# A gated cross-attention block on one core: keys of the first batch in three groups, row units spread over steps 0 and 1, the last batch divided per token, gates spread by matmul

## The chip, the cores and the metric

The kernel runs on one core of a Trainium2 chip. Its engines are TensorE (PE, matmuls; PEld are its weight loads), VectorE (DVE), ScalarE (ACT), GpSimd (POOL) and SyncE (SP), which here only issues DMAs. The metric is the device time of one execution in microseconds. Three executions of the kernel before took 1306.92, 1310.46 and 1322.75 us: the median is 1310.46.

## What is computed

The input x has 16 batches of 256 tokens of width 128; the context has 16 batches of 1601 keys of width 128. Cross-attention with 16 heads of depth 8, then a mixture of 8 experts (2 per token) with a shared expert, each behind a tanh gate:

```python
x = x + tanh(g_xattn) * attention(v=ctx, k=ctx, q=layernorm(x))
x = x + tanh(g_ffn) * ffn(layernorm(x))
# attention: softmax(qh @ kh.T / sqrt(8)) @ vh per head, then the dense projection
# ffn: scores = sigmoid(x @ gate_W) * route_scale; the top 2 of 8, normalised to sum 1,
#      weigh the experts gelu(x @ W1 + b1) @ W2 + b2; a shared expert is added
```

## The kernel before

A **step** is one group of eight heads (four pairs) of one batch: 32 steps, two per batch. A **chunk** is 512 tokens, that is two batches: 8 chunks. All that happens follows one list of events per step, ORDER[s], written as letters in PLAN; every engine walks through the same list and waits on counting semaphores.

The events:
- **S**, a row unit (`row_scores`, `maximum`): TensorE makes scores of 128 tokens against 512 keys for the two heads of a pair, in one of two b_ps banks, and VectorE takes their maxima. A step needs 26 of them: 24 of 512 keys and two for the 65 keys that are left. They run a step and ten units ahead (S_AHEAD).
- **T**: when the maxima of a step are complete they are negated, split in three bf16 parts, transposed by TensorE, copied by ScalarE into nm_t, and SyncE sends them as extra rows of q_op (`move_maxima`, 6 DMAs). Only then can the step's probabilities be made.
- **P**, a score pair: TensorE makes scores of 128 keys by 256 tokens with the maximum already taken off (four matmuls into two of three a_ps banks), ScalarE takes their exponential, 512 wide, into probs.
- **V** and **W**: TensorE multiplies probs with values into o_ps. Columns of ones in v_op also give the sums of the softmax. The last one of a step is followed by ScalarE's copy of o_ps into o_s.
- **A** units share the a_ps ring: K (project keys), V (project values), QT and QP (transpose and project normalised tokens), T, FT, FL, FG, FH (the feed-forward part: transpose, gate logits, transpose of gates, hidden layer). FH uses Gelu, P uses Exp: each change loads a table on ScalarE.
- **B** and **Y/Z** units share b_ps with S: D is the dense projection of a batch, Y and Z the two halves of the feed-forward output of 128 tokens.

Queries and keys are split into three bf16 parts, stored to memory (q_dram, k_dram) and loaded back in another layout (q_op, k_op, `load_operands`), four buffers deep. The keys of batches 1 to 15 are split by GpSimd (`split_keys`), those of batch 0 by VectorE (`split_run`), and the queries by GpSimd (`split_queries`). kctx and vctx hold one batch of context each, in one buffer each, so a load waits for the last projection from it.

The beginning, PROLOGUE, projects the keys of batch 0 in four runs of about 400 and the queries of chunk 0. VectorE and GpSimd fill k_op with ones first, because three rows of it have to stay one. SyncE stores all keys, ScalarE's queue all queries, and SyncE loads both. Then 26 row units run for step 0, T, the value projections of batch 0, QT and QP of chunk 1 and ten row units of step 1; after that come the first P.

The end: after the last P and V of step 31, the outputs of the last step go to memory (o_dram) and come back as num (the products) and den (the sums); den is inverted by VectorE, goes to memory once more (r_dram), comes back spread over the 128 partitions (den_all), and GpSimd multiplies (`divide`). The dense projection follows, then the output of chunk 6 (four Y/Z), the normalising of chunk 7 on GpSimd, its gates, whose result goes to memory and comes back spread (`spread_gates`, g_all), the hidden layer, GpSimd's product of both (`apply_gates`) and four Y/Z.

SyncE's queue is in order. In its loop over the steps it sends outputs, stores keys, loads operands, loads vctx, spreads sums and gates, moves maxima, loads kctx and stores queries, each behind a wait; what stands behind a wait has to wait too.

## Time and profile before

| | us |
|---|---|
| median of three executions | 1310.46 |
| profiled execution, its own time | 1312.06 |
| its span | 1310.3 |
| TensorE busy | 1183.9 (90%) |
| VectorE busy | 1068.6 (82%) |
| ScalarE busy | 1049.8 (80%) |
| GpSimd busy | 372.3 (28%) |

The page gives the busy time of each engine over the span and in 40 slices of 32.8 us. The timeline gives instructions in order of time, neighbours of one kind merged (x4: four instructions); an "SPq" or "ACTq" row is the issue of DMAs by that engine's queue. In brackets is how long the engine had been idle before, and what ended that. The chain is followed back from the last instruction to what released it at each step. The clock is the one granted to TensorE: 1.00 is 2.4 GHz, 0.50 is 1.2 GHz.

### The profile page before, as it was taken

How to read it: one execution, taken by the hardware profiler on the slowest of the kernel's cores; microseconds unless marked ns; L12 is line 12 of the kernel's file. 1: busy time of each engine (PE TensorE's matmuls, PEld its weight loads, DVE VectorE, ACT ScalarE, POOL GpSimd, SP SyncE). 2: the span in 40 equal slices, each digit the busy share in tenths (PEclk: the TensorE clock that was granted, in tenths of full speed). 3: DMA queues.
4: the chain of work that ended last, by engine and by line, in shares of the span. 5: the costliest groups of instructions: out<-in, count | busy, mean ns of one | idle time of the engine just before them, and what ended most of it. 6: DMA issues, size and time to landing. Idle time of an engine off the chain costs nothing.

```text
span 1310.3 us, 30858 instructions
## 1 busy us (share of the span) xinstructions
PE 1183.9 (90%) x11995; PEld 455.4 (35%) x11995; DVE 1068.6 (82%) x1337; ACT 1049.8 (80%) x1962; POOL 372.3 (28%) x361
## 2 busy tenths in 40 slices
PE   2369899989999999999999999999999999999854
PEld 1123333333333433343334433343333433343223
DVE  8478888989889898989898898879898899989011
ACT  1017897989998899988998899878998899889931
POOL 7424041421425042422424042422424032000111
PEclk7558998999999999999999999999999999999977
DMA  5854452635464654626363655636373654400101
GB/s 133 201 120 94 103 113 62 142 76 123 96 139 94 134 120 101 138 66 130 80 150 77 139 118 104 132 73 123 75 155 77 139 118 104 87 13 26 43 15 49
DMA packets 64100, 133.71 MB, mean 102 GB/s; under 512 B 13769, under 2 KB 38034, under 8 KB 60882
## 3 DMA queue, kind: packets, MB, share of 16 engines
q1 hardware_dynamic: 63090, 130.95, 46.2%
q8 instruction: 95, 1.56, 0.5%
q10 hardware_dynamic: 864, 0.79, 0.3%
q14 instruction: 51, 0.42, 0.1%
HBM read 87.91 MB, written 43.40 MB: 100 GB/s over the span
## 4 chain that ended last, share of the span: by engine, by line
PE 75%; DVE 10%; DMA 6%; ACT 5%; issue 2%; POOL 1%; SPq 1%; ACTq 0%; POOLq 0%; DVEq 0%
PE o_ps L792 30%; PE a_ps L774 18%; PE b_ps L758 13%; DVE run_max L917 7%; PE a_ps L706 5%; DMA vctx<-ctx_t 3%; PE a_ps L702 3%; ACT probs L586 3%; PE b_ps L737 2%; PE a_ps L698 1%; PE b_ps L726 1%; PE a_ps L685 1%; ACT L601 1%; DMA q_op<-q_dram 1%; PE b_ps L740 1%
## 5 line engine op out<-in xcount | busy, mean ns | idle before, releaser
L917 DVE TENSOR_REDUCE run_max<-b_ps 128x2 f32<-128x1024 f32 x768 | 899.0, 1218 | 126.0 <-PE b_ps L758 118.2
L586 ACT ACTIVATE probs<-a_ps 128x512 f32<-128x512 f32 (+1 forms) x1664 | 901.9, 595 | 105.2 <-PE a_ps L774 90.8
L792 PE MATMUL o_ps<-probs,v_op 128*32 128x256 f32 (+1 forms) x5368 | 501.9, 445 | 1.4 <-ACT probs L586 0.6
L758 PE MATMUL b_ps<-k_op,q_op 48*128 48x512 bf16 (+1 forms) x2048 | 317.1, 342 | 43.5 <-DVE run_max L917 24.6
L774 PE MATMUL a_ps<-q_op,k_op 51*128 51x256 bf16 (+1 forms) x3328 | 327.8, 275 | 18.7 <-ACT probs L586 15.0
L774 PEld LDWEIGHTS a_ps<-q_op,k_op 51*128 51x128 bf16 (+1 forms) x3328 | 108.0, 96 | 347.1 <-ACT probs L586 302.7
L792 PEld LDWEIGHTS o_ps<-probs,v_op 128*32 128x32 f32 x5368 | 107.4, 108 | 186.2 <-issue 113.0
L758 PEld LDWEIGHTS b_ps<-k_op,q_op 48*128 48x128 bf16 x2048 | 87.1, 95 | 164.9 <-DVE run_max L917 93.3
L488 POOL TENSOR_TENSOR k_parts<-k_t,one 128x400 bf16<-128x400 f32 (+1 forms) x60 | 51.4, 856 | 182.8 <-ACT k_t L607 182.8
L499 POOL TENSOR_TENSOR rstd_q<-rstd_q,minus_half 128x4 f32<-128x4 f32 x8 | 8.7, 1085 | 290.3 <-DVE rstd_q L850 290.3
L528 POOL TENSOR_TENSOR attn<-num,den_all 128x256 f32<-128x256 f32 x16 | 11.7, 729 | 236.7 <-PE b_ps L758 151.8
L607 ACT ACTIVATE k_t<-a_ps,bk_s 128x401 f32<-128x401 f32 (+1 forms) x64 | 38.4, 601 | 41.6 <-PE a_ps L702 41.2
L706 PE MATMUL a_ps<-wv_s,vctx 128*128 128x128 f32 (+1 forms) x416 | 63.9, 295 | 8.5 <-DMA vctx<-ctx_t 7.4
L702 PE MATMUL a_ps<-kctx,wk_s 128*128 128x400 f32 (+1 forms) x128 | 64.1, 594 | 5.9 <-DMA bk_s<-bk 5.9
L706 PEld LDWEIGHTS a_ps<-wv_s,vctx 128*128 128x128 f32 (+1 forms) x416 | 51.6, 194 | 27.7 <-ACT probs L586 15.0
L490 POOL TENSOR_TENSOR k_t<-k_t,k_parts 128x400 f32<-128x400 f32 (+1 forms) x60 | 56.9, 948 | 4.7
L494 POOL TENSOR_TENSOR k_parts<-k_t,k_parts 128x400 bf16<-128x400 f32 (+1 forms) x60 | 53.6, 893 | 4.7
L488 POOL TENSOR_TENSOR q_parts<-q_t,one 128x512 bf16<-128x512 f32 x8 | 8.4, 1045 | 161.9 <-ACT q_t L624 161.9
L492 POOL TENSOR_TENSOR k_parts<-k_t,one 128x400 bf16<-128x400 f32 (+1 forms) x60 | 51.0, 850 | 4.7
L612 ACT ACTIVATE v_op<-a_ps 128x512 f32<-128x512 f32 x64 | 33.0, 518 | 19.5 <-PE a_ps L706 19.0
L920 DVE TENSOR_REDUCE run_max<-b_ps 128x8 f32<-128x520 f32 x64 | 41.7, 694 | 3.3 <-PE b_ps L758 3.1
L534 POOL TENSOR_TENSOR hid<-hid,g_all 128x2048 f32<-128x2048 f32 x8 | 36.3, 4537 | 25.4 <-DMA g_all<-g_dram 17.6
(101 smaller groups left out, 612.0 us busy)
## 6 DMA issues: line engine op xcount, KB each, us to landing
k_op<-k_dram SPq DMA_DIRECT2D x64, 400.2 KB, 7.3
k_dram<-k_parts SPq DMA_DIRECT2D x32, 600.4 KB, 6.6
kctx<-ctx_t SPq DMA_DIRECT2D x16, 800.5 KB, 4.7
k_op<-k_dram SPq DMA_DIRECT2D x64, 200.1 KB, 7.8
vctx<-ctx_t SPq DMA_DIRECT2D x16, 800.5 KB, 11.0
o_dram<-o_s SPq DMA_DIRECT2D x32, 256.0 KB, 2.0
g_all<-g_dram SPq DMA_DIRECT2D x16, 512.0 KB, 6.0
k_dram<-k_parts SPq DMA_DIRECT2D x32, 200.1 KB, 5.8
```

What stands on the lines that cost most here:

```text
L488: pool.tensor_tensor(parts[0], whole, ones(whole, slice(0, whole.shape[0])), ALU.mult).then_inc(chain, 1)
L490: pool.tensor_tensor(whole, whole, parts[0], ALU.subtract).then_inc(chain, 1)
L492: pool.tensor_tensor(parts[1], whole, ones(whole, slice(0, whole.shape[0])), ALU.mult).then_inc(chain, 1)
L494: pool.tensor_tensor(parts[2], whole, parts[1], ALU.subtract).then_inc(chain, 1)
L586: act.activation(probs[0:keys, unit % PB, :], a_ps[at % AB][0:keys, :], ACT.Exp, scale=SCALE).then_inc(a_taken, 1)
L702: last = pe.matmul(bank[:, 0:n_keys], wk_s[:, :], kctx[:, k0:k0 + n_keys], start=True, stop=True)
L706: last = pe.matmul(bank[0:KEYS[t], 128 * (t % 4):128 * (t % 4) + 128], vctx[:, 128 * t:128 * t + KEYS[t]], wv_s[:, :], start=True, stop=True)
L758: last = pe.matmul(slot[:, side, to:to + n_keys], q_op[buf][rows, p, 128 * t:128 * t + 128], k_op[buf][rows, p, k0:k0 + n_keys], start=Tru ...
L774: last = pe.matmul(a_ps[(at + side) % AB][0:KEYS[t], SEQ * a:SEQ * a + SEQ], k_op[buf][rows, slot, 128 * t:128 * t + KEYS[t]], q_op[buf][r ...
L792: last = pe.matmul(o_ps[32 * j:32 * j + 32, cols], v_op[s // 2 % 2][0:KEYS[t], t, GP * (s % 2) + j, :], probs[0:KEYS[t], unit % PB, cols], ...
L917: dve.tensor_reduce(run_max[:, t, :, p, c:c + 1].rearrange("q v o -> q (v o)"), slot[:, :, :], AX.X, ALU.max).then_inc(b_taken, 1)
L920: dve.tensor_reduce(run_max[:, i - FULL, :, :, RUNS], slot[:, :, 0:GP * REST].rearrange("q v (p k) -> q v p k", p=GP), AX.X, ALU.max).then ...
```

## The change

It has two parts, at the beginning and at the end; steps 2 to 30 keep their lists.

**The beginning.** The context of batch 0 comes in three loads (512, 512 and 577 keys), the tokens of chunk 0 behind the first. Keys are projected in runs of 512, 512, 512 and 65 (KRUN_0). VectorE splits run 0, then the queries, then run 1; GpSimd splits runs 2 and 3. SyncE stores and loads the keys by group, in the order 0, 2, 1. The queries' stores are shared by ScalarE's queue (side 0) and GpSimd's queue (side 1), and GpSimd's queue also issues the two loads of step 0's queries. Ones are no longer filled by VectorE and GpSimd in k_op; a row of ones (k_row, 3 by 1601) is sent by eight DMAs. Step 0's 26 row units take key group 0 first, then 2, then 1 (`score_run`). The value projections of batch 0 and the key projections of batch 1 stand among them. The ten row units ahead are gone from there: six stand in step 0 and four in step 1 (`with_more_maxima`), and QT, QP of chunk 1 stand in step 0. The bias of values is folded behind T of step 0, in o_ps instead of b_ps.

**The end.** The output of chunk 6 stands in step 31's list. For batch 15 nothing goes to memory: the copied o_s is transposed by TensorE (unit OT, for step 30's half during step 31), VectorE inverts the sums and multiplies per token (`divide_tokens`), TensorE transposes back (unit AT), ScalarE copies, dense follows. Statistics of tiles 0 and 1 of chunk 7 are taken earlier, VectorE normalises chunk 7. The hidden layer stands ahead of the gates' transpose. The gates are spread by four matmuls with a constant pick_s, VectorE multiplies each quarter of hid, and the output's groups accumulate over the quarters in b_ps (`last_output`).

```diff
+KRUN_0 = [(RUN * c, RUN) for c in range(RUNS)] + [(RUN * RUNS, REST)]
+GROUPS = [(0, RUN), (RUN, RUN), (2 * RUN, CTX - 2 * RUN)]
+FIRST_RUNS = [0, 2, 1]
...
 def first_maxima():
...
+    events = [("S", n) for n in range(SUNITS)]
+    for i in range(4):
+        events.insert(events.index(("S", 3 * i + 3)), ("A", ("V", 0, i)))
+        events.insert(events.index(("S", 2 * i + 15)), ("A", ("K", 1, i)))
+    return events, [("A", ("T", 0, 0))]
...
+ORDER[0] = with_more_maxima(0, SUNITS, 6)
+ORDER[1] = with_more_maxima(1, 2 * SUNITS + 6, 4)
+ORDER[0].insert(len(ORDER[0]) // 4, ("A", ("QT", 1, 0)))
+ORDER[0].insert(len(ORDER[0]) * 2 // 5, ("A", ("QP", 1, 0)))
...
+    during = ORDER[STEPS - 1]
+    during.insert(len(during) // 3, ("B", ("OT", 0, 0)))
+    for i in range(4):
+        at = len(during) * (9 + i) // 14
+        during[at:at] = [("Y", ("FY", c - 1, i)), ("Z", ("FY", c - 1, i))]
+    ORDER[STEPS] = [e for e in ORDER[STEPS] if e[0] in "VW"] + [("B", ("OT", 1, 0)), ("A", ("AT", b, 0)),
+                                                               ("B", ("D", b, 0))]
+    ORDER[STEPS + 1] = [("A", ("FT", c, 0)), ("A", ("FL", c, 0))]
+    ORDER[STEPS + 2] = [("A", ("FH", c, i)) for i in range(GELU_TILES + 1)] + [("A", ("FG", c, 0))]
...
 # SyncE
-            store_keys(0)
-            load_operands(0)
+            store_group(0)
+            load_group(0)
+            store_group(2)
+            store_group(1)
+            load_group(2)
+            load_group(1)
             load_context("K", kctx, 1, kctx_in)
...
                 if s % 2 == 1 and 0 < b + 2 < BATCH:
                     store_keys(b + 2)
+                if s == -1:
+                    move_maxima(0)
                 if 2 <= s + 3 < STEPS:
                     load_operands(s + 3)
...
 # GpSimd
+            for i in (2, 3):
+                split_first_run(pool, k_second, i, 4 * (i - 2),
+                                lambda part, whole: pool.tensor_tensor(part, whole, ones(whole), ALU.mult))
+            store_queries(pool, 0, [1], q0_written)
+            load_queries(pool, 0, q0_in)
+            for i in range(2):
+                pool.memset(v_op[i][:, :, :, 16:32], 1.0).then_inc(v_ones, 1)
...
 # VectorE, the end
+            def divide_tokens(h):
+                unit = b_ps[B_SLOT["OT", h, 0]][:, 0, :].rearrange("q (i j r) -> q i j r", i=4, r=32)
+                dve.wait_ge(b_filled, b_done("OT", h))
+                dve.reciprocal(sum_inv[:, :, :], unit[:, :, :, 16]).then_inc(inv_seq, 1)
+                dve.wait_ge(inv_seq, h + 1)
+                for side in range(2):
+                    last = dve.tensor_tensor(attn_tok[:, :, side, h], unit[:, side::2, :, DH * side:DH * side + DH],
+                                             sum_inv[:, side::2, :].unsqueeze(3).broadcast_to([128, QTILES, GP, DH]),
+                                             ALU.mult)
+                last.then_inc(b_taken, 1)
+            def last_output():
+                for m in range(GELU_TILES):
+                    dve.wait_ge(pick_filled, m + 1)
+                    dve.tensor_tensor(hid[:, m, :], hid[:, m, :], a_ps[m % AB][:, :], ALU.mult).then_inc(pick_taken, 1)
```

**SyncE, from the six token loads on, before.** The waits in brackets are semaphores: k_chain is the split of batch 1's keys, a_taken the copy of step 0's maxima.

```order
L337 DMA x_s<-x 128x512 x6
L427 DMA k_dram<-k_parts 64x3x1601 [waits k_chain]
L429 DMA k_dram<-k_parts 64x1601
L427 DMA k_dram<-k_parts 64x3x1601
L429 DMA k_dram<-k_parts 64x1601
L362 DMA k_op<-k_dram 32x6404 [waits q_written,k_written,k_ones2]
L362 DMA k_op<-k_dram 16x6404
L364 DMA q_op<-q_dram 48x4x256
L362 DMA k_op<-k_dram 32x6404
L362 DMA k_op<-k_dram 16x6404
L364 DMA q_op<-q_dram 48x4x256
L437 DMA q_op<-nm_t 1x4x256 [waits a_taken]
```

And of the change, from the same place on:

```order
L455 DMA x_s<-x 128x512 x6
L551 DMA k_dram<-k_parts 64x3x1601 [waits k_chain]
L553 DMA k_dram<-k_parts 64x1601
L551 DMA k_dram<-k_parts 64x3x1601
L553 DMA k_dram<-k_parts 64x1601
L579 DMA q_op<-nm_t 1x4x256 [waits a_taken]
L579 DMA q_op<-nm_t 1x4x256 x5
L484 DMA k_op<-k_dram 32x6404 [waits k_written]
```

The maxima rows of step 0 have moved ahead of step 2's operands, and stay behind the store of batch 1's keys. kctx of batch 2 follows step 2's operands.

**TensorE, from T of step 0 (into 24 columns' rows, nm_parts) to the first key projection of batch 2 (kctx, 128x401), before.** b_ps rows are row units (two matmuls each), rows of four a_ps<-q_op,k_op are one P.

```order
L712 MATMUL a_ps<-ident_b,nm_parts 24x128 x2
L706 MATMUL a_ps<-wv_s,vctx 128x128 x4
L682 MATMUL a_ps<-ident,xn_q 128x128 x4
L706 MATMUL a_ps<-wv_s,vctx 128x128 x8
L706 MATMUL a_ps<-wv_s,vctx 65x128
L758 MATMUL b_ps<-k_op,q_op 128x512 x10
L685 MATMUL a_ps<-xn_t_q,wq_s 128x512
L758 MATMUL b_ps<-k_op,q_op 128x512 x10
L774 MATMUL a_ps<-q_op,k_op 128x256 x4
L758 MATMUL b_ps<-k_op,q_op 128x512 x2
L774 MATMUL a_ps<-q_op,k_op 128x256 x4
L758 MATMUL b_ps<-k_op,q_op 128x512 x2
```

And of the change:

```order
L883 MATMUL a_ps<-ident_b,nm_parts 24x128 x2
L831 MATMUL o_ps<-ident,bv_p 128x128
L833 MATMUL o_ps<-wd_s,bv_t 128x128
L992 MATMUL a_ps<-q_op,k_op 128x256 x4
L974 MATMUL b_ps<-k_op,q_op 128x512 x2
L992 MATMUL a_ps<-q_op,k_op 128x256 x4
L974 MATMUL b_ps<-k_op,q_op 128x512 x2
L992 MATMUL a_ps<-q_op,k_op 128x256 x4
L974 MATMUL b_ps<-k_op,q_op 128x512 x2
L873 MATMUL a_ps<-kctx,wk_s 128x401
```

Ten row units, the value projections and QT, QP stand no longer between T and the first P; the two matmuls of the bias do.

**TensorE, from the last product with values to the end, of the change.** Before, dense, four output groups, FT, FL, FG, five FH and four output groups stood here in this order, without the rows of o_s, attn_tok and pick_s.

```order
L910 MATMUL b_ps<-ident,o_s 128x128 x4
L852 MATMUL a_ps<-ident,attn_tok 128x128 x2
L900 MATMUL b_ps<-wd_s,attn 128x128 x2
L845 MATMUL a_ps<-ident,xn_f 128x128 x4
L857 MATMUL a_ps<-gate_s,xn_t_f 128x8 x4
L866 MATMUL a_ps<-xn_t_f,w_s 128x512 x4
L866 MATMUL a_ps<-xn_t_f,ws_s 64x512
L862 MATMUL a_ps<-ident,g_tok 8x128 x4
L922 MATMUL a_ps<-hid_s,pick_s 128x512
L937 MATMUL b_ps<-ws_s,hid_s 128x128 x4
L922 MATMUL a_ps<-hid_s,pick_s 128x512
L928 MATMUL b_ps<-w_s,hid 128x128 x4
```

The first four output groups have moved up into step 31, and the hidden layer ahead of the gates' transpose.

## Rows read from the trace of the kernel before

**Rows 1.** The page, the granted clock in 40 slices of the span:

```profile
PEclk7558998999999999999999999999999999999977
```

**Rows 2.** Busy time by stretch: start:end, length, busy us of each engine, clock, DMA:

```profile
102.50:141.00 38.50, 36.68 (x344) 13.44 (x342) 31.34 (x32) 30.86 (x59) 14.14 (x16) 0.94 0.37 73
141.00:174.60 33.60, 29.30 (x342) 9.40 (x338) 29.72 (x31) 29.90 (x58) 0.00 (x0) 1.00 0.59 128
1224.00:1259.00 35.00, 27.97 (x312) 7.23 (x308) 0.00 (x0) 32.28 (x62) 0.00 (x0) 1.00 0.03 11
1300.00:1305.00 5.00, 4.81 (x22) 4.81 (x23) 0.49 (x2) 0.00 (x0) 0.14 (x1) 0.50 0.02 5
1305.00:1310.00 5.00, 2.44 (x20) 2.25 (x18) 0.92 (x3) 0.00 (x0) 0.00 (x0) 0.95 0.14 52
```

**Rows 3.** Timeline of the beginning up to the first row unit: start, us, engine, line:

```profile
7.45 0.81 DVE L843 BATCH_NORM_STATS2 stats_q<-x_s 128x6 f32<-128x128 f32 x4
9.64 0.37 DVE L946 CAST k_parts<-k_t 128x401 bf16<-128x401 f32 x1 [0.77 <-ACT k_t L607]
10.66 1.09 DVE L950 CAST k_parts<-k_t 128x401 bf16<-128x401 f32 x1
15.33 0.69 ACT L624 ACTIVATE q_t<-a_ps,bq_s 128x512 f32<-128x512 f32 x1 [1.28 <-PE a_ps L685]
19.82 1.36 POOL L494 TENSOR_TENSOR q_parts<-q_t,q_parts 128x512 bf16<-128x512 f32 x1
21.22 7.69 ACTq L321 DMA_DIRECT2D q_dram<-q_parts  x6
45.92 1.04 PE L758 MATMUL b_ps<-k_op,q_op 48*128 48x512 bf16 x4 [17.22 <-DMA q_op<-q_dram]
```

**Rows 4.** Timeline on to the first P and K2.0; last row: DMAs, us to landing:

```profile
52.12 4.98 PE L702 MATMUL a_ps<-kctx,wk_s 128*128 128x401 f32 x8
57.46 21.59 DVE L917 TENSOR_REDUCE run_max<-b_ps 128x2 f32<-128x1024 f32 x19 [3.68 <-PE b_ps L758]
69.14 0.89 POOL L494 TENSOR_TENSOR k_parts<-k_t,k_parts 128x400 bf16<-128x400 f32 x1
73.68 1.12 SPq L429 DMA_DIRECT2D k_dram<-k_parts  x1
79.52 0.80 SPq L362 DMA_DIRECT2D k_op<-k_dram  x2
82.30 3.85 SPq L437 DMA_DIRECT2D q_op<-nm_t  x6
86.20 0.44 SPq L417 DMA_DIRECT2D kctx<-ctx_t  x1
98.91 0.63 PE L774 MATMUL a_ps<-q_op,k_op 51*128 51x256 bf16 x4
102.48 1.71 PE L702 MATMUL a_ps<-kctx,wk_s 128*128 128x401 f32 x2
...
kctx<-ctx_t SPq DMA_DIRECT2D x1, 800.5 KB, 7.7
```

**Rows 5.** The chain that ended last, its end, and one row of ScalarE's timeline:

```profile
1258.97 0.60 ACT o_s L594
1280.64 0.20 ACT score L626
1284.69 0.20 DVE g_tok L887
1286.08 0.59 ACT hid_s L631
1288.83 6.68 DMA g_all<-g_dram
1307.48 0.35 DVE y_s L904
...
1291.77 0.68 ACT L635 ACTIVATE hid_s<-a_ps,bs_s 64x512 f32<-64x512 f32 x1 [0.32 <-PE a_ps L698]
```

More of the change, by code:

```diff
@@ L146, in first_maxima, with with_more_maxima, last_steps @@
 def first_maxima():
-    scores = [event for event in ORDER[-2] if event[0] == "S"]
-    rest = [event for event in ORDER[-2] if event[0] != "S"]
-    first = [event for event in ORDER[-1] if event[0] == "S" and event[1] < SUNITS]
-    turn = [("A", ("T", 0, 0))]
-    return scores[:5] + rest + scores[5:], first + turn + [e for e in ORDER[-1] if e not in first + turn]
-ORDER[-2], ORDER[-1] = first_maxima()
+    events = [("S", n) for n in range(SUNITS)]
[3 more added lines that the diff above has]
+    return events, [("A", ("T", 0, 0))]
+def with_more_maxima(s, n, more):
+    turn, last = ("A", ("T", s + 1, 0)), SUNITS * (s + 2) - 1
+    events, seen, due = [], 0, 0
+    for kind, unit in ORDER[s]:
+        if kind == "S":
+            events.append(("S", n))
+            n, seen = n + 1, seen + 1
+            due += seen % (SUNITS // more) == 0 and seen // (SUNITS // more) <= more
+        elif (kind, unit) != turn:
+            events.append((kind, unit))
+            if kind == "P" and due:
+                events.append(("S", n))
+                n, due = n + 1, due - 1
+    events.insert(events.index(("S", last)) + 5, turn)
+    return events
+ORDER[-2], ORDER[-1] = first_maxima()
+ORDER[0] = with_more_maxima(0, SUNITS, 6)
+ORDER[1] = with_more_maxima(1, 2 * SUNITS + 6, 4)
+ORDER[0].insert(len(ORDER[0]) // 4, ("A", ("QT", 1, 0)))
+ORDER[0].insert(len(ORDER[0]) * 2 // 5, ("A", ("QP", 1, 0)))
+def last_steps():
+    c, b = CHUNKS - 1, BATCH - 1
+    during = ORDER[STEPS - 1]
[7 more added lines that the diff above has]
+    ORDER[STEPS + 2] = [("A", ("FH", c, i)) for i in range(GELU_TILES + 1)] + [("A", ("FG", c, 0))]
+    for s in range(STEPS + 3, LAST + 1):
+        ORDER[s] = []
+last_steps()
 def step_of(unit):
@@ L329, in load @@
                 return sp.dma_start(dst[tuple([slice(None)] * len(src.shape))], src)
-            load(kctx, ctx_t[0]).then_inc(kctx_in, 16)
-            for dst, src in keys:
-                load(dst, src).then_inc(key_in, 16)
             def load_tokens(c0, c1, arrived):
@@ L469, in _ @@
                     sp.dma_start(out[:, 4 * c:4 * c + 4, :], y_s[:, :, :]).then_inc(out_done, 16)
-            sp.wait_ge(out_done, 16 * CHUNKS)
+            for i in (0, 2):
+                sp.wait_ge(y_done, i + 2)
+                sp.dma_start(out[:, TILES - 4 + i:TILES - 2 + i, :], y_s[:, i:i + 2, :]).then_inc(out_done, 16)
+            sp.wait_ge(out_done, 16 * (CHUNKS + 1))
         @block.gpsimd
@@ L685, in a_unit @@
                     last = pe.matmul(bank[:, :], wq_s[:, :], xn_t["q"][:, :], start=True, stop=True)
+                elif kind == "AT":
+                    pe.wait_ge(b_taken, b_done("OT", 1))
+                    for t in range(QTILES):
+                        last = pe.transpose(bank[:, 128 * t:128 * t + 128],
+                                            attn_tok[:, t].rearrange("q s h j d -> q (s h j d)"), ident[:, :])
                 elif kind == "FL":
@@ L837, in fold_bias, with statistics @@
                 dve.wait_ge(bias_seq, 4)
-            def statistics(w, c):
+            def statistics(w, c, tiles=range(4)):
                 seq = lambda k: dve.wait_ge(bn_seq[w], 6 * c + k)
-                for t in range(4):
+                for t in tiles:
                     dve.bn_stats(stats[w][:, t, :], x_s[:, 4 * c + t, :]).then_inc(bn_seq[w], 1)
+                if tiles[-1] < 3:
+                    return
                 seq(4)
@@ L1005, in _ @@
                     gates = []
+            last_output()
 def kernel(**inputs):
```

336 lines of the change are left out of this document (238 added, 98 removed).

## The prediction

> **What bounds the kernel now.** I read the page first, then the busy time by stretch, then the timelines of the beginning and the end. TensorE's clock row is at the full level in the middle slices and lower in the first four and the last two [rows 1]: the change works on exactly these two ends. In the middle three engines are close together: between 102.5 and 174.6 us TensorE is busy 66.0 of 72.1 us, VectorE 61.1, ScalarE 60.8 [rows 2]. A row unit (two matmuls, one VectorE maximum) moved into a step therefore meets no idle engine. Step 31, the last, has no row units: ScalarE is busy 32.3 of 35 us, TensorE 28.0, VectorE 0 [rows 2].
>
> Beginning, to be read as a chain: token statistics 7.45, queries projected 15.33 + 0.69, split on GpSimd until 21.18, stored by ScalarE's queue until 28.9, and the first row unit at 45.92 [rows 3]. Then 26 row units, the key projection of batch 1 at 52.12, its split until 70.03, its store until 74.8, maxima rows sent from 82.30, and the first probabilities' matmul only at 98.91 [rows 4]. Between 82.3 and 98.9 stand value projections and ten row units for step 1. The end is one chain of 51.3 us, from the last copy of sums at 1258.97 to the span's end at 1310.3 [rows 5]; 24 us of it lie behind the gates' copy at 1286.08.
>
> **Step A, the first row unit.** Tokens are loaded ahead of most keys and VectorE no longer fills k_op: the statistics can begin when the tokens land instead of at 7.45. 800 KB of keys now come in three loads and only the first is ahead of the tokens; I take 5.3, a gain of 2.2. The projected queries are then ready at 16.0 - 2.2 = 13.8. VectorE splits them in four operations instead of GpSimd's 5.1 us (16.02 to 21.18). The same cast took 0.37 us alone and 1.09 beside a GpSimd operation [rows 3]; GpSimd now splits key group 2 at that time, so four operations cost between 2.5 and 5; I take 4.4, because GpSimd is busy for most of it: ready at 18.2, before at 21.18. The Trainium skill (SBUF — State Buffer, Who interferes with whom) says that a VectorE cast in its two-port mode and a GpSimd operation lock each other out for the whole instruction; the two casts agree with this.
>
> From ready queries to the first row unit took 24.7 us before [rows 3]. ScalarE's six stores took 7.69; now three go there and three on GpSimd: -3.8. The load needs the queries and one third of the keys, not all keys, and has a queue of its own. No row shows a DMA issued by GpSimd. Its price lies between ScalarE's 1.28 us per issue and, if five of them stand in line behind other work, some 3 us each. I take 14.8 us from ready to first row unit: **33 us** (28 to 42; 42.9 if the stretch stays 24.7). Before: 45.9. The key groups come after that: group 2 is needed 8 units later, group 1 16 units later, and I put their landing at 36 and 41, 8 us early.
>
> **Step B, from there to step 0's first key projection.** A row unit costs VectorE 21.59/19 = 1.136 us [rows 4]. Four value projections (about 2.1 us at the low clock) and four key projections now stand among them; two banks hold 2.3 us of VectorE's work, so each costs 0 to 0.8: 2.4 in sum. Batch 1's first key projection comes after 15 units: 33 + 17.0 + 2.4 = 52.4. Before it was at 52.12. From there the same work follows: 17.9 us to the end of the split, 4.8 to the end of the store [rows 4]. The maxima of step 0 are ready at 33 + 26 units + 2.4 + 0.9 = 65, before at 81.9. But SyncE now has the store of batch 1's keys ahead of the maxima rows, and waits there for GpSimd's split, to 70.3. The rows leave at 75.1 to 79 and the first probabilities' matmul is at about 80.5 instead of 98.9. The gap of 15 us between 65 and 80 is this change's new wait.
>
> Second wait: the first three pairs of step 0 take 3.6 us (98.91 to 102.48), then TensorE wants keys of batch 2 (K2.0). Their load is issued behind the operands of step 2, which wait for the keys' store to land (4.7 us after its last issue) and take 2.7: 82.5, before at 86.20. It landed 7.7 us after issue [rows 4]; right behind 1.4 MB of operand loads I add 1.8: 92. TensorE gets there at 84 and stands 8 us, with everything queued behind it: the row units, so VectorE, and the pairs, so ScalarE. K2.0 at 92 against 102.48: **-10.5**. Both waits hang on GpSimd's split and move with step A.
>
> **Step C, ten row units in steps 0 and 1, with QT and QP of chunk 1.** In TensorE's time a row unit is about 0.32 us in the dense part: 3.2, and the query projection about 1.5: 4.7. In VectorE's time ten cost 11.4 us, against 7.2 + 3.9 idle in the two stretches [rows 2]. So at least +4.7, at most +11.4; both engines end near full, which they never pack: I take **+7**. At the end of step 1: -10.5 + 7 = -3.5.
>
> **Step D, the end.** All of chunk 6's outputs (4 groups of ten matmuls; 20 matmuls took 2.44 us at 0.95 of the clock [rows 2], so 1.2 each) and one transpose unit go into step 31, whose TensorE has 7 us idle; four bunches in a ring of three banks, so not for nothing: +1.5 (0 to 5). After the last sums: copy 0.60, transposes 0.65, reciprocal and two products 0.8, transposes and copy 0.95, dense 1.0, add 0.5, statistics of two tiles 1.15, power 1.1, four normalising operations on VectorE 0.9, transposes 0.65, copy 0.7, logits 1.15, exponential 0.25: 10.4. Hidden layer now ahead of the gates' copy: from the table load to the last Gelu 5.8 us (1286.7 to 1292.45), which hides the 4.0 us of gate arithmetic (1280.84 to 1284.88); the copy 0.6: 16.8. Then four spreading matmuls, four products of 0.7 and 20 output groups: TensorE's 8.4 us at the full clock, up to 15 at the low one. Output groups ran at a granted clock of 0.50, the 1.2 GHz level, in 1300 to 1305, after 6 us without TensorE work, and at 0.95, nearly all at 2.4 GHz, behind that [rows 2]; I take 9.8: 26.6. Last addition 0.35, output 2.15: **29.1** (27.5 to 33), before 51.3. Gone are the trips through memory: 9 us for sums and 9 us for gates (6.68 of it one row) and the 4.5 us GpSimd product. D: -22.2 + 1.5 = **-20.7**.
>
> The Trainium skill (TensorE: Matmul & The Clock Gate, Part 1) says that the low clock is the default and activity lifts it; by this rule the end, now denser, would take 27.5 to 29 us. The rows of 1300 to 1310 agree with it.
>
> **Sum.** -3.5 - 20.7 = -24.2 from the profiled execution's own 1312.06: 1287.9. The median of the runs shown is 1.6 lower: **1286 us**, 1.9% less.
>
> **Rivals.**
> (1) Faster than that: GpSimd's DMAs cost like ScalarE's and queries land early (first unit at 28, -5), row units fill idle time (+4.7 instead of +7), the end at 27.5 (-1.6), step 31 takes its guests free (-1.5): 1286 - 10.4 = 1276. For it: VectorE is idle 11 us in the two stretches of steps 0 and 1 [rows 2]. Against: both waits of step B, which stay in this case too.
> (2) GpSimd's DMAs are slow, the first unit at 42, and step B moves with it: 1286 + 9 + 2 = 1297. The Trainium skill (SBUF — State Buffer, SBUF: two separate sides) says that a VectorE copy in two-port mode keeps GpSimd from writing descriptors. Here VectorE's casts of key group 1 run just then; five issues each held for one cast of 1.09 us are 5.5 us late.
> (3) Chunk 6 in step 31 isn't hidden and the end stays at the low clock: +3.5 and +4: 1293.
> (4) Slower than before: the same queue as in (2), but starved until the key stores are over. Everything hangs on it one for one; it decides from a first row unit at 33 + 24 = 57 us, 11 later than before. At 84, which 2% slower needs, nothing in the trace points.
>
> **How the numbers follow.** Forecast 0.48, (1) 0.27, (2) 0.13, (3) 0.09, (4) 0.03. The range reaches from (1) with 3 us more to (2) with 2 more: 1273 to 1299. 2% of 1310.46 is 26 us (about what a measurement of this kernel can tell), so the border is 1284.3. Above 2% faster: all of (1) and 0.15 of the forecast, whose own range is 1279 to 1293: 0.42. Slower by 2%: 0.01. The rest 0.57.
>
> **What would show it.** Step A: the first row unit at 28 to 42. B: SyncE's store of batch 1's keys ahead of the maxima rows, VectorE idle from about 65 to 80, TensorE waiting for kctx near 84 to 92. C: sums' copy of step 1 at 171, before 174.6. D: 29 us from the last sums' copy to the end. If VectorE has no gap at 65, B is wrong and the time is below 1280; if the end takes over 35 us, D is.

## The result and the profile after

The changed kernel takes 1306.15 us in the median of 20 runs (1300.64 to 1315.73), the kernel before 1315.69 in 20 runs beside it (1306.92 to 1328.52): the ratio is 0.9932, 95% interval 0.9912 to 0.9953. Forecast were 24 us less; it is 9.5, or 0.7%. The profiled execution took 1310.04 us (span 1308.2); the one before had 1312.06, so these two traces differ by 2.0 us only.

The timeline of the beginning, kernel after (start, us, engine, line; to be read beside [rows 3, 4]):

```profile
13.35 0.69 ACT L788 ACTIVATE q_t<-a_ps,bq_s 128x512 f32<-128x512 f32 x1 [1.28 <-PE a_ps L848]
24.63 1.18 POOL L428 DMA_DIRECT2D q_op<-q_dram  x2 [3.47 <-DMA q_dram<-q_parts]
28.74 1.04 PE L974 MATMUL b_ps<-k_op,q_op 48*128 48x512 bf16 x4 [15.43 <-DMA q_op<-q_dram]
...
70.32 6.18 SPq L579 DMA_DIRECT2D q_op<-nm_t  x6
78.16 0.61 PE L992 MATMUL a_ps<-q_op,k_op 51*128 51x256 bf16 x4 [11.87 <-DMA q_op<-nm_t]
79.23 3.79 DVE L1175 TENSOR_REDUCE run_max<-b_ps 128x2 f32<-128x1024 f32 x3 [10.49 <-PE b_ps L974]
90.34 1.68 PE L873 MATMUL a_ps<-kctx,wk_s 128*128 128x401 f32 x2 [8.59 <-DMA kctx<-ctx_t]
133.95 0.60 ACT L756 ACTIVATE o_s<-o_ps 128x512 f32<-128x512 f32 x1
174.15 0.60 ACT L756 ACTIVATE o_s<-o_ps 128x512 f32<-128x512 f32 x1
```

The first row unit comes 17 us sooner and batch 2's first keys (K2.0) 12.1 us sooner. The last two rows, the copies of the sums of steps 0 and 1, tell what is left: 7.1 us at the end of step 0 (141.04 before) and 0.4 us at the end of step 1 (174.58).

The timeline of the end, kernel after (to be read beside [rows 5]):

```profile
1269.44 0.60 ACT L756 ACTIVATE o_s<-o_ps 128x512 f32<-128x512 f32 x1 [1.26 <-PE o_ps L1010]
1278.55 1.09 PE L845 MATMUL a_ps<-ident,xn_f 128*128 128x128 f32 x4 [4.18 <-DVE xn_f L1083]
1282.11 6.31 PE L866 MATMUL a_ps<-xn_t_f,w_s 128*128 128x512 f32 x8
1290.17 0.58 ACT L795 ACTIVATE hid_s<-a_ps 8x512 f32<-8x512 f32 x1
1290.81 1.12 PE L922 MATMUL a_ps<-hid_s,pick_s 8*128 8x512 f32 x2 [0.85 <-ACT hid_s L795]
1295.81 2.07 PE L922 MATMUL a_ps<-hid_s,pick_s 8*128 8x512 f32 x2
1301.81 3.78 PE L928 MATMUL b_ps<-w_s,hid 128*128 128x128 f32 x16
```

From the last copy of sums to the span's end are 38.8 us (51.3 before). The same spreading matmul took 1.12 us at 1290.81 and 2.07 at 1295.81. Busy time by stretch of this end (start:end, length, busy us, clock, DMA):

```profile
1268.00:1270.00 2.00, 1.06 (x8) 0.16 (x8) 0.00 (x0) 0.74 (x2) 0.00 (x0) 1.00 0.00 0
1276.00:1278.00 2.00, 0.00 (x0) 0.00 (x0) 0.81 (x4) 0.00 (x0) 1.01 (x1) 0.50 0.00 0
1292.00:1294.00 2.00, 2.00 (x11) 1.12 (x11) 0.66 (x1) 0.00 (x0) 0.00 (x0) 1.00 0.00 0
1296.00:1298.00 2.00, 2.00 (x3) 0.50 (x4) 0.09 (x1) 0.00 (x0) 0.00 (x0) 0.50 0.00 0
```

The granted clock is 0.50 (1.2 GHz) from 1270.4 to 1287.4 and again from between 1294 and 1295 to the end, the second time although TensorE has had work without a gap since 1290.81. Step 31 takes 33.6 us (28.9 before), and steps 2 to 30 together 1061.7 against 1055.5.

### The profile page after: what moved, and what is told of

Same layout as the page of the kernel before. It is cut to its first block, busy times and chain, and to the rows that moved or that the text cites. A ratio compares the mean times of both kernels' runs of the same rounds, so it can differ in the third digit from the quotient of the medians.

```text
span 1308.2 us, 30941 instructions
## 1 busy us (share of the span) xinstructions
PE 1200.6 (92%) x12013; PEld 460.2 (35%) x12013; DVE 1060.5 (81%) x1343; ACT 1051.0 (80%) x1963; POOL 357.3 (27%) x366
## 4 chain that ended last, share of the span: by engine, by line
PE 71%; DVE 8%; DMA 6%; issue 5%; ACT 3%; POOL 3%; SPq 2%; POOLq 0%; ACTq 0%; DVEq 0%
PE o_ps L1010 27%; PE a_ps L992 16%; PE b_ps L974 12%; DVE run_max L1175 6%; PE a_ps L877 5%; DMA vctx<-ctx_t 3%; PE a_ps L873 3%; ACT probs L748 2%; PE a_ps L866 2%; PE b_ps L951 2%; DMA kctx<-ctx_t 1%; DMA r_dram<-den 1%; PE b_ps L900 1%; ACT L763 1%; PE a_ps L857 1%
## 5 line engine op out<-in xcount | busy, mean ns | idle before, releaser
L992 PE MATMUL a_ps<-q_op,k_op 51*128 51x256 bf16 (+1 forms) x3328 | 328.6, 276 | 30.0 <-ACT probs L748 14.8
L873 PE MATMUL a_ps<-kctx,wk_s 128*128 128x400 f32 (+3 forms) x128 | 66.3, 604 | 13.0 <-DMA kctx<-ctx_t 8.6
L877 PEld LDWEIGHTS a_ps<-wv_s,vctx 128*128 128x128 f32 (+1 forms) x416 | 53.0, 198 | 30.2 <-issue 17.4
L769 ACT ACTIVATE k_t<-a_ps,bk_s 128x401 f32<-128x401 f32 (+2 forms) x64 | 38.4, 602 | 22.1 <-PE a_ps L873 21.6
L866 PE MATMUL a_ps<-xn_t_f,w_s 128*128 128x512 f32 x64 | 34.1, 661 | 1.1 <-ACT hid L797 0.3
## 6 DMA issues: line engine op xcount, KB each, us to landing
vctx<-ctx_t SPq DMA_DIRECT2D x16, 800.5 KB, 10.8
```

The costliest lines, as they stand in the source:

```text
L866: last = pe.matmul(to, w, xn_t["f"][:, :], start=True, stop=True)
L873: last = pe.matmul(bank[:, 0:n_keys], wk_s[:, :], kctx[:, k0:k0 + n_keys], start=True, stop=True)
L877: last = pe.matmul(bank[0:KEYS[t], 128 * (t % 4):128 * (t % 4) + 128], vctx[:, 128 * t:128 * t + KEYS[t]], wv_s[:, :], start=True, stop=True)
L992: last = pe.matmul(a_ps[(at + side) % AB][0:KEYS[t], SEQ * a:SEQ * a + SEQ], k_op[buf][rows, slot, 128 * t:128 * t + KEYS[t]], q_op[buf][r ...
```

## Experiments

Times are medians, with the ratio to before and its 95% interval. Before was run again beside each kernel (medians 1313.37 to 1317.03 us), so kernels are compared by the ratios. The changed kernel's own ratio is 0.9932 (0.9912 to 0.9953); where another's interval overlaps this one, the whole time doesn't tell the two apart, and what is said rests on a part of one profile of each. "Sums 1" is the start of the copy of step 1's sums; "tail" runs from the copy of step 31's sums to the span's end.

### Which end brought the gain

```diff
-last_steps()
...
-            last_output()
```

With these two calls goes all that serves the new end; before's end stands in its place.

> The changed kernel with its old end: the last batch divided by the spread sums, the gates spread through DRAM, chunk 6's outputs in step 33, last normalisation on GpSimd; the beginning is the new one. Theory (from the two traces): the beginning is worth little by the end of step 1 (174.15 us against 174.58), so this kernel stands within 3 us of before (1310 to 1316 in the medians), its sums of step 1 are copied at 173 to 175, its step 31 takes 28.9 us again instead of 33.6, and its tail is about 51 us. The end is then worth 6 to 9 us. Rival: the end gave nothing (its tail's 12 us are eaten by step 31 and by the low clock) and the beginning the 9 us: this kernel would stand at 1304 to 1308.

Measured: 1314.49 us, ratio 1.0003 (0.997 to 1.0036). Sums 1 at 173.28, step 31 28.87 us, tail 51.7. The beginning alone is worth nothing that shows, and its interval lies clear of the changed kernel's: the end brought the 0.7%, 12.9 us in the tail less 4.7 in step 31. The rival, 1304 to 1308 us, is refuted.

### The beginning: ten units, and the wait for kctx

```diff
-ORDER[0] = with_more_maxima(0, SUNITS, 6)
-ORDER[1] = with_more_maxima(1, 2 * SUNITS + 6, 4)
+ORDER[0] = [("S", n) for n in range(SUNITS, SUNITS + S_AHEAD)] + ORDER[0]
```

> The changed kernel, but the ten row units ahead stand in front of step 0 (between the turn of the first maxima and the first scores) as they did before, instead of being spread over steps 0 and 1. Theory: steps 0 and 1 are lengthened by these ten units (43.6 and 40.2 us against 38.6 and 33.5 before), and VectorE's idle 10.5 us ahead of the first scores takes them for nothing: steps 0 and 1 go back to about 39 and 34 us, the clock doesn't fall at 168 to 178 us, and the end of step 1 comes 8 to 11 us sooner (163 to 166), the whole 8 to 11 us faster than the changed kernel. Rival: the steps are longer for another reason (the wait for kctx, transfers, the clock), or the ten units delay the first scores as much as they save: end of step 1 within 2 us of 174, whole within 0.3%.

The second edit, kctx_early, loads batch 2's context ahead of the store of batch 1's keys (and no longer behind step 2's operands):

```diff
+                if s == -1:
+                    load_context("K", kctx, 2, kctx_in)
                 if s % 2 == 1 and 0 < b + 2 < BATCH:
                     store_keys(b + 2)
```

> The changed kernel, with the load of batch 2's context (kctx) issued ahead of the store of batch 1's keys instead of behind the loads of step 2's operands. Theory: TensorE's 8.59 us wait at the first keys of batch 2 (90.34 us) goes: those keys at 81 to 83, the end of step 0 7 to 8.6 us sooner (125 to 127 against 133.95). By the end of step 1 the rest of it may be lost again, since VectorE's row units fill that step: 166 to 170 against 174.15, whole 4 to 8 us faster. Rival: the wait is taken over by the next one (VectorE's row units, or the keys' copy): end of step 1 within 2 us, whole the same.

The sums' copies, first two rows of ten_in_gap, in the second fence of kctx_early, whose K2.0 stands ahead of them:

```profile
130.55 0.60 ACT L755 ACTIVATE o_s<-o_ps 128x512 f32<-128x512 f32 x1
164.08 0.60 ACT L755 ACTIVATE o_s<-o_ps 128x512 f32<-128x512 f32 x1
```

```profile
82.67 1.71 PE L875 MATMUL a_ps<-kctx,wk_s 128*128 128x401 f32 x2
126.20 0.60 ACT L758 ACTIVATE o_s<-o_ps 128x512 f32<-128x512 f32 x1
166.39 0.60 ACT L758 ACTIVATE o_s<-o_ps 128x512 f32<-128x512 f32 x1
```

ten_in_gap: 1298.64 us, ratio 0.9897 (0.9854 to 0.994). Step 1 is 33.5 us again and sums 1 comes 10.1 us sooner (8 to 11 expected). From K2.0 to sums 1 are 74.0 us (90.05 to 164.08) instead of 83.8: this is what the ten units cost in these two steps, 9.8 us, the fall of the clock behind them (below) included. kctx_early: 1298.91, ratio 0.9889 (0.9846 to 0.9931). K2.0 no longer waits, and both copies come 7.8 us sooner: nothing of it is lost by the end of step 1. In the profiles both theories hold at the sizes expected. In the whole time each interval overlaps the changed kernel's; only both edits together (all_three, below) are clear of it.

Is it VectorE that the ten units cost, or TensorE? Two kernels with cheaper maxima. VectorE reads only half of the columns, in half_max for 20 units and in half_wide for all 62 units of steps 0 and 1 (there `if SUNITS <= n < 3 * SUNITS + 10`):

```diff
-... slot[:, :, :],
+                    seen = RUN // 2 if 0 <= n - SUNITS < 10 or 0 <= n - 2 * SUNITS - 6 < 10 else RUN
+... slot[:, :, 0:seen],
```

> The changed kernel, but twenty row units (the first ten that run in step 0 and the first ten of step 1's list) are reduced by VectorE over half their columns, about 0.55 us each instead of 1.09; TensorE's matmuls and the order stay. The row maxima then miss half of those keys (the subtracted number is another, which the division takes out again). Theory: the ten units added to steps 0 and 1 cost their full time on VectorE, 43.6 + 40.2 against 38.6 + 33.5 us before, since VectorE is busy in nearly every window of these steps: with 5.5 us less for VectorE in each, step 0 is 3.5 to 5.5 and step 1 3.5 to 6 us shorter (end of step 1 at 163 to 167 against 174.15). Rival: TensorE's share of the units (0.39 us each, and the waits of the scores queued behind them) lengthens the steps: end of step 1 at 172 to 174.

Measured: 1307.26, ratio 0.9918 (0.9891 to 0.9946); sums 1 at 173.12, 1.0 us sooner only, and K2.0 1.5 us sooner, so from K2.0 on nothing is gained. My theory missed. VectorE's busy time fell from 76.8 to 67.8 us between 78 and 182, and TensorE's waits for row maxima hardly changed (3.8 us, 4.0 in the changed kernel): they stand at other units. The reason may be that the two banks hand VectorE at most two units ahead, so that time saved at a unit that nobody waits for isn't kept for later ones; no run shows this by itself.

> The changed kernel, but all 62 row units that run in steps 0 and 1 are reduced by VectorE over half their columns (0.55 us instead of 1.09), not only the first ten of each step; the row maxima then miss half of those keys (the subtracted number is another, which the division takes out again). The run before (twenty units) moved nothing, with TensorE's waits for VectorE at 3.8 us as before: they stand at other units. Theory: of the 11.7 us by which steps 0 and 1 are longer, TensorE's waits for VectorE's row units are about 4 us and the fall of the clock behind the last of them 2 to 3; the rest is TensorE's own matmuls of the ten units. With all units at half time the waits go, the clock stays up: step 1 35 to 37 us instead of 40.2, step 0 1 to 2.5 us shorter, end of step 1 at 166 to 170. Rival: TensorE's own work and order is all of it: end of step 1 at 172 to 174.

TensorE's waits for row maxima between 98 and 166 us, in the changed kernel and in half_wide (us in total, times, longest):

```profile
PE b_ps L974 <- DVE run_max L1175: 4.0, 9, 0.9
```

```profile
PE b_ps L974 <- DVE run_max L1176: 0.6, 2, 0.4
```

Measured: 1295.37, ratio 0.9868 (0.9837 to 0.9899); sums 1 at 162.87, 11.3 us sooner, more than my 4 to 8. Step 1 took 34.4 us, 0.9 above before's, the clock stayed at 1.00 behind its last bunch, and K2.0 came 2.6 us sooner. From K2.0 to sums 1 are 75.1 us, 8.7 less than in the changed kernel and 3.0 more than before. So the larger part of the lengthening hangs on VectorE's time; my expectation had given nearly half of it to TensorE's own matmuls. VectorE's price of the ten units alone can't be read from this run: all 62 units were shortened, so part of the 8.7 us is time that before paid as well. Here the whole time too is clear of the changed kernel's.

Behind the last bunch of units the clock fell (168 to 178). In step1_busy the matmuls of step 1's last four row units are done three times, to fill TensorE's waits there:

```diff
-for p, to, k0, n_keys in parts:
+for p, to, k0, n_keys in parts * (3 if 3 * SUNITS + 6 <= n < 3 * SUNITS + 10 else 1):
```

> The changed kernel, but the last four row units of step 1's list (units 84 to 87, behind which TensorE waited 0.5 to 0.7 us each for VectorE) do their matmuls three times over before VectorE may read them, with the same values. Theory: step 1 lasts 40.2 us and not 36 to 37 because TensorE's waits at these units let the granted clock fall to 0.50 from 168 to 178 us; with the waits filled the clock stays at 1.00 and step 1 takes 36.5 to 38.5 us, step 2 1 us less. Rival: VectorE's row units hold the step's end, and the fall of the clock hits where nothing waits for TensorE, or comes anyway: step 1 stays at 39.5 to 41 us.

Stretches of the changed kernel, and in the second fence of step1_busy:

```profile
166.00:168.00 2.00, 0.74 (x8) 0.18 (x4) 2.00 (x3) 1.07 (x2) 0.00 (x0) 0.96 0.53 218
168.00:170.00 2.00, 2.00 (x10) 0.30 (x10) 2.00 (x2) 0.00 (x0) 0.00 (x0) 0.50 0.00 0
```

```profile
166.00:168.00 2.00, 1.67 (x16) 0.65 (x16) 2.00 (x3) 1.07 (x3) 0.00 (x0) 1.00 0.75 301
168.00:170.00 2.00, 1.69 (x16) 0.37 (x14) 2.00 (x3) 0.39 (x1) 0.00 (x0) 1.00 0.00 0
```

Measured: 1305.04, ratio 0.9915 (0.9882 to 0.9948), not told apart from the changed kernel. The clock stayed at 1.00, step 1 took 38.3 us instead of 40.2 and step 2 39.3 instead of 40.7. That fits, but is not shown by it: of six profiles of kernels with exactly the changed kernel's beginning, four had the fall (step 1 40.2 us in the changed kernel, begin_only, warm_tail and spread73) and two had not (37.9 in y_late and after_again). The fall costs about 2.3 us in step 1 and 1 to 3 in step 2, and whether it comes differs from run to run, with the kernel unchanged too (the changed kernel and after_again).

### Step 31 and the tail

```diff
-        during[at:at] = [("Y", ("FY", c - 1, i)), ("Z", ("FY", c - 1, i))]
...
+    ORDER[STEPS + 2][-1:-1] = late[0] + late[1]
+    ORDER[STEPS + 2] += late[2] + late[3]
```

Units 0 and 1 stand behind the hidden matmuls, 2 and 3 behind the gates' turning (FG). The last chunk's hidden values go to g_all and its gates to a tensor of their own (end_s), because chunk 6's are still in use.

> The changed kernel, but chunk 6's outputs are computed in the tail, where TensorE waits for the GELUs and the gates, not in step 31; the last chunk's hidden values and gates then lie in tensors of their own (g_all, and one more) so that chunk 6's are not overwritten. Theory: in step 31 TensorE is full already (about 1.08 us a pair of scores), so four bunches of 1.3 us lengthen it by 4.7 us (33.6 against 28.9); in the tail they are hidden. Step 31 goes back to 28.9 to 29.5 us, the tail stays at 38.8 (+0 to 1.5), whole 3.5 to 5 us faster. Rival: step 31 is long because VectorE or the turning of the sums holds it, or the tail grows by as much: whole within 1.5 us.

Measured: 1302.43, ratio 0.9906 (0.9872 to 0.9941). Step 31 took 28.89 us: chunk 6's four bunches cost all of the 4.7 us. But the tail grew from 38.8 to 42.6, more than I allowed: at the low clock TensorE had no gap behind the hidden matmuls (1270.19 to 1277.5 in one run of work), so the units pushed the gates' turning from 1277.5 to 1279.8 and the first spreading behind that. Of the 4.7 us gained, 3.8 are lost again, and the ratio doesn't tell this kernel from the changed one. This profile holds one thing more. From 1270.19 on TensorE works without a gap, and the clock comes back to 1.00 at 1276; it falls all the same at 1286, some 3 us after the first spreading matmul (1282.58):

```profile
1284.00:1286.00 2.00, 2.00 (x11) 1.12 (x10) 0.55 (x2) 0.00 (x0) 0.00 (x0) 0.96 0.30 113
1286.00:1288.00 2.00, 2.00 (x9) 1.78 (x10) 0.56 (x1) 0.00 (x0) 0.00 (x0) 0.50 0.00 0
```

In warm_tail 22 matmuls whose result nobody reads stand in the tail's waits:

```diff
+def keep_busy(times):
+    for _ in range(times):
+        pe.matmul(o_ps[:, :], ident_b[:, :], k_parts[:, 0, 0:512], start=True, stop=True)
```

> The changed kernel with matmuls added in the tail whose result nobody reads (bf16, 128 rows by 512 columns, into the bank of the sums, which is free by then): 2 after each turning of the sums and of the attention, 10 after the last dense product, 2 after the turned normalised tokens, 1 after the gates' turning, 1 ahead of each of the four groups of the output. Theory: the tail is 38.8 us and not 29 because TensorE's granted clock fell to 0.50 as soon as TensorE waited between 1269 and 1278, and the tail's matmuls then took twice the time; kept busy it stays at 1.00, the hidden matmuls take about 3.7 us instead of 7.4, the tail is 30 to 33 us, the whole 6 to 9 us faster. Rival: the clock falls in the tail for another reason (the kind of matmuls that run there), or the chain of ScalarE and VectorE holds the tail: the clock falls all the same, the tail stays at 38 to 43 us, the whole is the same or up to 3 us slower for the added matmuls.

```profile
1274.00:1276.00 2.00, 1.65 (x12) 1.18 (x12) 0.00 (x0) 0.60 (x1) 0.00 (x0) 0.95 0.00 0
1276.00:1278.00 2.00, 2.00 (x6) 1.44 (x7) 0.86 (x4) 1.18 (x2) 0.00 (x0) 0.50 0.00 0
1290.00:1292.00 2.00, 2.00 (x7) 1.47 (x7) 0.00 (x0) 0.00 (x0) 0.00 (x0) 0.50 0.00 0
```

Measured: 1305.79, ratio 0.9928 (0.9898 to 0.9957), tail 39.3 us: nothing. These are stretches of warm_tail. The clock was at 1.00 again from 1270, behind the added matmuls. After 2.03 us without work ahead of 1273.9 and 0.35 more it fell before the hidden matmuls, and it fell a second time just before 1290 in the output's part, where TensorE had been at work without a gap since 1285.7. Waits alone don't explain the tail. What differs there is the kind of matmul: the spreading has 8 rows of operands. So spread73 gives it 72, the 64 added ones against zeros:

```diff
-pe.matmul(a_ps[m % AB][:, :], pick_s[HID:HID + EXPERTS, m, :], g_t, ...)
+pe.matmul(a_ps[m % AB][:, :], pick_w[:, m, :], hid_s[0:HID + EXPERTS, :], ...)   # upper 64 rows zero
```

> The changed kernel, but the last chunk's gates are spread by matmuls over 72 rows (the 8 rows of gates and the 64 above them, against zeros) instead of over 8; columns, count and result are the same. Theory: in the tail the granted clock falls to 0.50 at 1294 although TensorE is busy in every window, because the matmuls there use few of the rows; with 72 rows it stays at 1.00 to the end, and the output's part (15.2 us from the first spreading to the last matmul) takes 9 to 11 us, the whole 4 to 6 us less. Rival: rows don't matter, it is the short matmuls of the output (128 columns, each with a load of weights) that let the clock fall, or the earlier waits: the clock falls at the same place, the whole is the same within 0.3%.

Timeline and stretches of spread73 (72 rows, in spite of the label):

```profile
1285.25 1.13 PE L926 MATMUL a_ps<-hid_s,pick_w 72*128 72x512 f32 x2 [0.85 <-ACT hid_s L798]
1290.61 1.02 PE L926 MATMUL a_ps<-hid_s,pick_w 72*128 72x512 f32 x2
1291.47 2.10 PE L932 MATMUL b_ps<-w_s,hid 128*128 128x128 f32 x16
```

```profile
1288.00:1290.00 2.00, 2.00 (x14) 1.52 (x13) 0.77 (x2) 0.00 (x0) 0.00 (x0) 1.00 0.00 0
1292.00:1294.00 2.00, 1.57 (x13) 1.30 (x11) 1.35 (x5) 0.00 (x0) 0.00 (x0) 1.00 0.00 0
```

Measured: 1299.00, ratio 0.9871 (0.9803 to 0.994); tail 32.4 us. From the first spreading to the last output matmul are 8.3 us instead of 14.8, at a clock of 1.00 throughout. As many matmuls with as many columns, only with 72 rows of operands instead of 8: the theory holds. The rival (the short output matmuls, or the earlier waits) falls: both are still there. The intervals of the whole time overlap, so this rests on the profiles, but on all of them: in the eleven with 8 rows the clock fell in this part every time (12.7 to 15.9 us), in the three with 72 rows (spread73, all73, all73_warm) never (8.2 to 8.3 us).

### The edits together

> The changed kernel with the ten row units ahead in front of step 0, batch 2's context loaded before batch 1's keys are stored, and chunk 6's outputs taken out of step 31 into waits of the tail (one behind the turned sums, two behind the last dense product, one behind the gates; last chunk's hidden values in tensors of their own). Theory: the three gains are of different causes, of which the first two share the wait ahead of step 0's keys: end of step 1 at 156 to 159 us (164.1 with the first alone, 166.4 with the second), step 31 28.9 us, tail 39 to 41 us, whole 15 to 20 us faster than the changed kernel in the medians. Rival: both edits of the beginning take away the same wait: end of step 1 at 163 to 165, whole 10 to 13 us faster.

Measured: 1283.43, ratio 0.9752 (0.9699 to 0.9806). Sums 1 at 155.00, 19.2 us sooner: the two gains of the beginning (10.1 and 7.8) add up, and this profile lacks the clock's fall in step 1. Step 31 took 30.2 us, not the 28.9 expected; the clock fell there at 1219 for some 4 us. The tail took 35.2, less than expected; its output's part was 12.7 us.

> As the kernel of three edits, and the first maxima's six transfers issued ahead of the store of batch 1's keys: they are ready at 64.3 us but issued at 70.3, behind a store that waits for GpSimd's split. Theory: first scores at 72 to 73 instead of 78.2, and step 1 ends 4 to 6 us sooner than with three edits. Rival: by then VectorE is at its ten row units until 76 us and holds the first steps anyway, or the store of the keys comes late for the operands of step 2: within 1.5 us of three edits.

Measured: 1282.43, ratio 0.9769 (0.9727 to 0.9811), sums 1 at 155.50: the rival. The six transfers left at 64.36, but TensorE waits for VectorE between the ten row units ahead of step 0, so the first scores came at 77.9 (77.4 in all_three).

> The kernel of three edits (ten units ahead of step 0, batch 2's context early, chunk 6's outputs in the tail) with the gates spread over 72 rows, the upper 64 of the matrix of picks set to zero in place. Theory: the clock stays at 1.00 in the output's part, which takes 8 to 9 us; tail 31 to 33 us against 35.2, whole 1277 to 1281, 24 to 30 us faster than the changed kernel in the medians. Rival: with chunk 6's output among the turned gates the clock fell at another place (1273.9) and for another reason: 1282 to 1285.

Measured: 1276.49, ratio 0.9709 (0.9675 to 0.9742), the fastest: 2.9% below before, the first with its whole interval more than 2% below, and by the two ratios some 2.2% below the changed kernel. From all_three its interval is not clear. In its profile the clock was at 1.00 from 1242 to 1256 and from 1264 to the end, tail 30.8 us; one fall stays, ahead of the hidden matmuls.

> As the kernel before it, and four added matmuls (bf16, 128 rows by 512 columns, nobody reads them): one after the turned attention, three after the turned normalised tokens. Theory: they fill the waits of 0.6 and 0.8 us after which the clock fell at 1260, the hidden matmuls run at 1.00 (about 4 us instead of 5.4 and 1.1), and the tail is 1 to 2.5 us shorter than without. Rival: the gates' product (8 columns a matmul) lets the clock fall by itself, or the GELUs and the gates' chain (4 us behind the scores) hold this part: within 0.5 us, or 0.5 us longer.

Measured: 1279.05, ratio 0.9733 (0.9698 to 0.9768): no gain. The hidden matmuls ran at 0.50 in 1258 to 1262 all the same. The waits of 0.6 and 0.8 us ahead of them were filled, so these are not what lets it fall there, or not alone. But the longest wait, 1.95 us for VectorE's normalised tokens, ends 1 to 2 us ahead of the fall in both kernels, and neither it nor the gates' product was tested alone; this is left open. The tail, 32.4 us, also holds a fall at its head (1247 to 1250) that all73's profile doesn't have.

> The changed kernel once more, for a second profile of it. Theory: the 4.8 us lost in its step 4 (a 3.4 us wait for vctx with the clock at 0.53 for 4 us) is the luck of one run, so step 4 is 36 to 37 us here and steps 2 to 30 together about 1057 us as in before, against 1061.7 in the first profile; step 1, with VectorE's last units, is either 38 (clock stays) or 40.2 us (clock falls), as in the kernels with the same beginning; step 31 33.6 us; tail 38 to 40 us. Rival: the change causes the loss of step 4: it is 41 us again.

Time of this run 1308.41. Step 4 took 36.8 us (41.2 in the first profile), steps 2 to 30 1055.7: the 6.2 us that the middle seemed to lose are luck of the first profile, 4.8 of them in step 4 and 1.5 in step 2, behind the fall at 168. But its step 31 took 38.6 us (33.6 in the first), because there the clock was low:

```profile
1238.00:1242.00 4.00, 4.00 (x22) 1.18 (x20) 0.04 (x1) 2.46 (x5) 0.00 (x0) 0.50 0.01 2
```

This fall lasted from 1231 to 1244 and cost 5.0 us; TensorE's waits around its start, up to 1.08 us, stand in the first profile too, without a fall. Step 4 of the first profile is another case. There TensorE first waited for vctx, and the clock fell in that wait, from 270 to 277:

```profile
271.56 2.05 PE L877 MATMUL a_ps<-wv_s,vctx 128*128 128x128 f32 x8 [3.37 <-DMA vctx<-ctx_t]
```

The same wait was 1.49 us in after_again, without a fall, and 3.79 in all73, whose step 4 took 41.4 us. So single profiles differ by more than some of the edits do.

## Why the prediction was right and wrong

What failed is above all step D. It took chunk 6's units as nearly hidden in step 31 (+1.5), and it priced the tail's matmuls at the full clock (29.1 us). The runs show +4.7 and, with the low clock in both halves of the tail, 38.8. Step C was mis-sized as well, by 4.7 us.

**Step A** put the first row unit at 33; it came at 28.74, in rival (1)'s place. Queries were ready at 14.0 (13.8 forecast), VectorE's split ended at 17.9 (18.2). From the split's end to the first unit it took 10.8 us, not 14.8: GpSimd's issues, the unknown, took 0.59 to 0.66 us each, as much as ScalarE's own 0.66 in this kernel and half of its 1.28 of before. Rival (2) never arose, and no issue of GpSimd's is seen to wait for a cast of VectorE's. One reading was loose: the cast of 0.37 us called alone (9.64) ran beside a small operation of GpSimd's (9.02 to 10.05, 128x4), so the trace agrees with a lock between the two only for the large ones.

**Step B** was right in its mechanism: the store of batch 1's keys ahead of the maxima rows, VectorE idle for 10.5 us, then TensorE's wait for kctx, 8.6 us (8 forecast). K2.0 came at 90.34, 12.1 us sooner (10.5 forecast). The runs add what the forecast left out: the gap of 10.5 us was the place for the ten units (ten_in_gap), and the second wait could be taken away by the order of one load (kctx_early). VectorE's gap was 10.5 us and not 15 because folding the bias and the statistics of chunk 1 came first, until 68.7, and the first scores came at 78.16 already (80.5 forecast).

**Step C** is a mis-sized term: +7 forecast, +11.7 measured (steps 0 and 1 from K2.0: 83.8 against 72.1). The forecast holds 5.5 us for the ten units and 1.5 for QT and QP. The ten units cost 9.8 us (ten_in_gap), and the 1.9 us that ten_in_gap still has above before are left for QT and QP. About 2.3 of the 9.8 are the clock's fall behind the last bunch, which no term held; without a fall (y_late, after_again) the two steps cost 8.4 and 10.7 us more than before, inside my bounds of 4.7 and 11.4. So the units themselves cost some 7.5 us, an estimate from these numbers, two thirds of VectorE's full time of 11.4. I had chosen by the average idle time of VectorE, 11 us, as if most of it could be used; about 4 us could. The end of step 1 gained 0.4 to 2.7 us in the six profiles, not 3.5, and where the clock fell step 2 gives most of it back or more: it ends 0.2 to 2.0 us later than before's (begin_only 0.3), where it didn't, 0.8 and 2.4 us sooner.

**Step D** holds most of the miss: -20.7 forecast, -7.9 measured (-12.6 in the tail, +4.7 in step 31).
- Step 31, 3.2 us: I counted 7 us idle in TensorE's row [rows 2]. But this time lies in pieces. A pair's scores and values mostly take TensorE 0.96 of the 1.08 us that ScalarE takes for them, which leaves gaps of 0.12 us, and its longer waits for ScalarE are five, of at most 1.1 us (3.8 in sum). Before:

```profile
1240.61 0.39 PE L774 MATMUL a_ps<-q_op,k_op 51*128 51x256 bf16 x4
1240.93 0.64 PE L792 MATMUL o_ps<-probs,v_op 128*32 128x256 f32 x8
1241.69 0.39 PE L774 MATMUL a_ps<-q_op,k_op 51*128 51x256 bf16 x4
```

  A bunch of 1.3 us fits into none of them. After the change ScalarE waits 1.12 us at a bunch; y_late, without them, is back at 28.89:

```profile
1256.85 2.17 ACT L748 ACTIVATE probs<-a_ps 128x512 f32<-128x512 f32 x4 [1.12 <-PE a_ps L992]
1260.13 2.16 ACT L748 ACTIVATE probs<-a_ps 128x512 f32<-128x512 f32 x4 [1.12 <-PE a_ps L992]
```

- Up to the gates' copy, 4.5 us (21.3 against 16.8): the steps came in the order forecast, at the low clock. 2.7 us lie up to the end of the scores' exponential (13.1 against 10.4), 1.8 between the table load and the last Gelu (7.6 against 5.8). I took before's rows of the full clock for matmuls that follow waits of 0.9, 0.8, 0.6 and 4.2 us. In all73, at 1.00 up to the logits, the first part took 11.6 us. Which wait lets the clock fall here stays open.
- The output's part, 5.0 us (14.8 against 9.8). I had the bounds, 8.4 and 15, and chose near the wrong one, arguing that TensorE is dense there. (Before's low clock in 1300 to 1305 stood behind 8.45 us without TensorE work, not the 6 that I read.) The Trainium skill's rule (TensorE: Matmul & The Clock Gate, Part 1), that activity lifts the clock, I had read as "busy is enough". The trace disagrees with that reading: 2.00 of 2 us busy at 0.50. spread73 shows what was missing: 8.3 us, just under my lower bound, with nothing changed but the rows.

With the clock up, step D's working was close: all73's tail is 30.8 us with all of chunk 6's units in it and one fall of the clock, forecast 29.1.

**The sum.** Between the two profiles the forecast misses by 22.2 us: 12.8 in D, 3.1 in A to C, 6.2 in the middle, which after_again doesn't repeat. In the medians (9.5 us gained, 24 forecast) the middle's share is gone and the others stand, 15.9 us together, against a miss of 15. Rival (3) had D's mechanism, chunk 6 not hidden and the end at the low clock, the end at less than half its size and 9% chance; it deserved the most. The sign and "within 2%" were right, the range was not.

## What to carry over

Idle time in a row of averages is not a place to put work. It can lie in pieces smaller than the work (step 31), or stand at places where the work can't use it (ten units cost some 7.5 of 11.4 us although 11 were idle). Before work is spread over full steps, look for the gap that the same change opens. Price the matmuls of a short end at both levels of the clock and ask what each does there: if they have few rows of operands, more rows (against zeros) may keep the clock up, as 72 in the place of 8 did here at no cost that shows.
